# Attention of an adaLN block on one core: scores and first softmax units started inside the value projection, normalising moved to GpSimd

## What is computed

```
mod = silu(c) @ wmod                        # six vectors of 1024 for each of 4 batches
h = layernorm(x) * (1 + ca) + sa            # x is 4 x 512 x 1024
q, k, v = h @ wq, h @ wk, h @ wv            # 32 query heads, 8 key/value heads of 128
q, k = rope(q), rope(k)
scores = q k^T / sqrt(128), masked to j <= i and j > i - 256
attn = softmax(scores);  out = attn v;  x = x + ga * (out @ wo)
h = layernorm(x) * (1 + cb) + sb
x = x + gb * (top-2 of 8 experts of rank 64, summed)
```

## Time and profile before

| | |
|---|---|
| median of 3 runs | 2964.62 us (2964.49 to 2965.58) |
| the profiled execution, its time | 2969.41 us |
| its span in the trace | 2967.6 us |
| PE busy | 2693.1 us (91%) |
| DVE busy | 1775.6 us (60%) |
| ACT busy | 1367.0 us (46%) |
| POOL busy | 853.6 us (29%) |
| mean granted TensorE clock | 0.971 of full |

### The profile page before, as it was taken

How to read it: one execution, slowest core, us unless ns; L and a number is a source line. 1 busy time by engine, 2 the same in 40 slices (tenths; PEclk the granted TensorE clock), 3 DMA queues, 4 the chain that set the end, 5 groups by cost and what they waited for, 6 DMA issues and landing times.

```text
span 2967.6 us, 40770 instructions
## 1 busy us (share of the span) xinstructions
PE 2693.1 (91%) x12889; PEld 2169.2 (73%) x12889; DVE 1775.6 (60%) x4070; ACT 1367.0 (46%) x2753; POOL 853.6 (29%) x364
## 2 busy tenths in 40 slices
PE   5799999998799999998799999998799999998999
PEld 3477777776577777776577777776577777776777
DVE  3455656566755565656755555567855556567443
ACT  3244444545444444454444444454444444445331
POOL 2133333231333333331333333231333333332212
PEclk8799999999899999999899999999899999999999
DMA  7522221212222222122222221222222222214211
GB/s 281 191 72 71 68 67 64 71 64 87 98 71 71 71 68 67 64 70 85 93 71 71 71 71 64 69 65 88 90 71 71 71 71 67 67 64 171 85 65 57
DMA packets 140548, 245.31 MB, mean 83 GB/s; under 512 B 7440, under 2 KB 74320, under 8 KB 139216
## 3 DMA queue, kind: packets, MB, share of 16 engines
q1 hardware_dynamic: 133520, 219.49, 22.3%
q10 hardware_dynamic: 6976, 25.20, 2.3%
HBM read 227.86 MB, written 16.81 MB: 82 GB/s over the span
## 4 chain that ended last, share of the span: by engine, by line
PE 51%; DVE 21%; issue 15%; ACT 9%; DMA 2%; DVEq 1%; ACTq 0%; POOL 0%; SPq 0%; POOLq 0%
PE bank L451 16%; PE bank L453 15%; PE bank L452 15%; PE bank L500 3%; DVE swapped L722 3%; DVE rotated L725 3%; DVE rotated L720 3%; DVE prob L766 3%; ACT qo_hi L610 3%; ACT swapped L605 3%; DVE prob L750 2%; ACT prob L650 1%; DVE qo_lo L740 1%; DVE acc L873 1%; DVE pT_lo L761 1%
## 5 line engine op out<-in xcount | busy, mean ns | idle before, releaser
L431 POOL TENSOR_TENSOR w_o_lo<-stage,w_o_hi 128x1024 fp32r<-128x1024 f32 x128 | 323.7, 2529 | 652.8 <-ACT w_o_hi L426 652.8
L451 PE MATMUL bank<-hT_hi,w_q_hi 128*128 128x512 f32 x1024 | 404.0, 395 | 19.8 <-POOL w_q_lo L431 19.3
L452 PE MATMUL bank<-hT_lo,w_q_hi 128*128 128x512 f32 x1024 | 401.5, 392 | 0.0
L451 PE MATMUL bank<-w_o_hi,qo_hi 128*128 128x512 f32 x1024 | 401.3, 392 | 0.0
L453 PE MATMUL bank<-hT_hi,w_q_lo 128*128 128x512 f32 x1024 | 401.1, 392 | 0.0
L452 PE MATMUL bank<-w_o_lo,qo_hi 128*128 128x512 f32 x1024 | 400.2, 391 | 0.0
L453 PE MATMUL bank<-w_o_hi,qo_lo 128*128 128x512 f32 x1024 | 400.1, 391 | 0.0
L604 ACT ACTIVATE swapped<-bank 64x512 f32<-64x512 f32 x160 | 95.3, 596 | 623.4 <-DVE rotated L720 623.4
L431 POOL TENSOR_TENSOR w_q_lo<-stage,w_q_hi 128x1024 fp32r<-128x1024 f32 x128 | 312.4, 2452 | 194.2 <-ACT w_q_hi L426 194.2
L431 POOL TENSOR_TENSOR w_v_lo<-stage,w_v_hi 128x1024 fp32r<-128x1024 f32 x32 | 76.8, 2399 | 1009.1 <-ACT w_v_hi L426 1009.1
L650 ACT ACTIVATE prob<-prob,nbias 128x384 f32<-128x384 f32 (+2 forms) x512 | 273.5, 534 | 178.8 <-DVE nbias L750 175.3
(11 more groups left out here) (179 smaller groups left out, 5510.3 us busy)
## 6 DMA issues: line engine op xcount, KB each, us to landing
stage<-in_wq SPq DMA_DIRECT2D x128, 512.0 KB, 3.6
stage<-in_wo SPq DMA_DIRECT2D x128, 512.0 KB, 3.3
stage<-in_wk SPq DMA_DIRECT2D x33, 512.0 KB, 3.7
xb<-in_x ACTq DMA_DIRECT2D x32, 512.0 KB, 5.3
stage<-in_wv SPq DMA_DIRECT2D x32, 512.0 KB, 3.6
acc<-in_wmod SPq DMA_DIRECT2D x32, 512.0 KB, 5.9
...
```

Source lines behind the costliest of these rows:

```text
L431: eng.tensor_tensor(dst[1], src, dst[0].bitcast(F32), ALU.subtract).then_inc(s_split, 1)
L451: eng.matmul(o, st[0], mv_[0], start=start, stop=False)
L452: eng.matmul(o, st[0], mv_[1], start=False, stop=False)
```

## The change

Seven edits, in the loop and, for the first group, in the code ahead of it:

- `act_rope` starts its half copies when the projection is done, and no longer after L720. `dve_rope` waits for those copies before L720.
- The copy of weight chunk 9 moves on ACT from rotation 4 to the end of rotation 3, ahead of rotation 4's half copies.
- PE issues S(0) and S(1), five chunks of V, S(2), and the other three chunks.
- DVE does the masks of units 0 and 1 ahead of rotation 4, and their reciprocals and the mask of unit 2 inside it; ACT does the two Exps inside it.
- The multiplication by the reciprocal is issued on POOL (`pool_normalise`), after the ten weight chunks of the group.
- In `pe_attention` step u is now T(u), the K chunk if there is one, S(u + 3), and values.
- `K_AT` is (0, 1, 2, 3, 5, 7, 12, 13) in place of (1, 2, 3, 5, 7, 12, 13, 14).

The edits of the first group's code (the same calls with `early` off, masks ahead of the memset) are left out of the diff.

```diff
@@ -45,6 +45,8 @@
 LA = 3
 LAG = 3
 V_TURN = LA + 2
+EARLY = 2
+V_SPLIT = 5
 
 
 def key_tiles(i):
@@ -445,6 +453,8 @@
             with eng.Fori(0, GROUPS) as n:
                 for j in range(NC):
                     pool_chunk(eng, n, j)
+                for u in range(UNITS):
+                    pool_normalise(eng, n, u)
 
 
         def mm3(eng, o, st, mv_, start, stop):
@@ -511,12 +521,16 @@
                 m = mm3(eng, OBANK[i % 2][:], sl(v_, lambda v: v[:, kt, :]), sl(pT[i % 2], lambda p: p[:, b, :]), b == 0, b == len(kts) - 1)
             m.then_inc(s_pv, 1)
 
-        K_AT = (1, 2, 3, 5, 7, 12, 13, 14)
+        K_AT = (0, 1, 2, 3, 5, 7, 12, 13)
 
         def pe_attention(eng, n, next_k):
             for u in range(UNITS):
-                if u + LA < UNITS:
-                    pe_scores(eng, n, u + LA)
+                pe_turn(eng, n, u)
+                if u == 1:
+                    eng.wait_ge(s_act, 7 * n + 6)
+                    for t in range(QT):
+                        m = eng.transpose(bank[7][:, t * P:(t + 1) * P], swapped[1][:, t * P:(t + 1) * P], ident_t[:])
+                    m.then_inc(s_vt, 1)
                 if next_k and u in K_AT:
                     k = K_AT.index(u)
                     if k == 0:
@@ -524,12 +538,8 @@
                     m = mm3(eng, bank[0][:], sl(w_k, lambda t: t[:, k, :]), sl(hT, lambda t: t[:, k, :]), k == 0, k == KT - 1)
                     if k == KT - 1:
                         m.then_inc(s_proj, 1)
-                pe_turn(eng, n, u)
-                if u == 1:
-                    eng.wait_ge(s_act, 7 * n + 6)
-                    for t in range(QT):
-                        m = eng.transpose(bank[7][:, t * P:(t + 1) * P], swapped[1][:, t * P:(t + 1) * P], ident_t[:])
-                    m.then_inc(s_vt, 1)
+                if u + LA < UNITS:
+                    pe_scores(eng, n, u + LA)
                 if u % GQ == 1 and GQ < u < UNITS - GQ:
                     pe_values(eng, n, u // GQ - 1)
             for i in (QT - 2, QT - 1):
@@ -549,9 +559,14 @@
                 waits = {2 * q: (s_split, 10 * n + 4 + q) for q in range(4)} if h == 0 else {}
                 pe_project(eng, n, f"Q{h}", w_q, slice(h * HD, (h + 1) * HD), 1 - h % 2, waits)
             eng.wait_ge(s_wor, 8 * n + 1)
-            for u in range(LA):
+            for u in range(EARLY):
                 pe_scores(eng, n, u)
-            pe_project(eng, n, "V", w_v, slice(0, HD), 1, {})
+            bank_free(eng, n, "V")
+            for k in range(KT):
+                if k == V_SPLIT:
+                    pe_scores(eng, n, EARLY)
+                m = mm3(eng, bank[1][:], sl(w_v, lambda t: t[:, k, :]), sl(hT, lambda t: t[:, k, :]), k == 0, k == KT - 1)
+            m.then_inc(s_proj, 1)
 
         def pe_ln_chunk(eng, b1, k, bk, depth=2):
 
@@ -593,21 +608,33 @@
         OUT_STEP = {GQ * i + GQ + 1 + LAG: i for i in range(QT - 2)}
 
 
-        def act_rope(eng, n, r):
+        def act_rope(eng, n, r, early=True):
 
             slot = r % 2
-            eng.wait_ge(s_dve, 5 * n + r + 1)
+            eng.wait_ge(s_proj, 6 * n + 2 + r)
             if r >= 2:
                 eng.wait_ge(s_qk, 5 * n + r - 1)
             half = HD // 2
             bk = bank[0 if r % 2 == 0 else 1]
             eng.activation(swapped[slot][0:half, :], bk[half:HD, :], ACT.Copy)
             eng.activation(swapped[slot][half:HD, :], bk[0:half, :], ACT.Copy).then_inc(s_act, 1)
-            if r:
+            if 1 <= r < GQ:
                 act_chunk(eng, n, 5 + r)
+            if r == GQ and early:
+                for u in range(EARLY):
+                    act_exp(eng, n, u)
             dst = kt_[0][:] if r == 0 else qo[0][:, r - 1, :]
             eng.wait_ge(s_ra, 5 * n + r + 1)
             eng.activation(dst, rotated[slot][:], ACT.Copy).then_inc(s_rh, 1)
+            if r == GQ - 1:
+                act_chunk(eng, n, NC - 1)
+
+        def act_exp(eng, n, u):
+            w = P * len(key_tiles(u // GQ))
+            tile = prob[:, u % GQ, 0:w]
+            eng.wait_ge(s_msk, UNITS * n + u + 1)
+            eng.activation(tile, tile, ACT.Exp, bias=nbias[:, u:u + 1], scale=-1.0,
+                           accum_out=rowsum[:, u:u + 1]).then_inc(s_exp, 1)
 
         def act_project(eng, n, batch_done=None):
 
@@ -643,12 +670,8 @@
                     nk = len(key_tiles(i))
                     eng.activation(pT[i % 2][0][:, 0:nk, h * P:(h + 1) * P],
                                    bank[5 + u % 2][:, 0:nk * P].rearrange("p (b q) -> p b q", q=P), ACT.Copy).then_inc(s_pth, 1)
-                if s < UNITS:
-                    w = P * len(key_tiles(s // GQ))
-                    tile = prob[:, s % GQ, 0:w]
-                    eng.wait_ge(s_msk, UNITS * n + s + 1)
-                    eng.activation(tile, tile, ACT.Exp, bias=nbias[:, s:s + 1], scale=-1.0,
-                                   accum_out=rowsum[:, s:s + 1]).then_inc(s_exp, 1)
+                if EARLY <= s < UNITS:
+                    act_exp(eng, n, s)
                 if s in OUT_STEP:
                     act_outputs(eng, n, OUT_STEP[s])
             for i in (QT - 2, QT - 1):
@@ -713,16 +736,23 @@
 
         LN_VAR = 3 * QT + 1
 
-        def dve_rope(eng, n, r):
+        def dve_rope(eng, n, r, early=True):
             slot = r % 2
             bk = bank[0 if r % 2 == 0 else 1]
+            if r == GQ and early:
+                for u in range(EARLY):
+                    dve_mask(eng, n, u)
             eng.wait_ge(s_proj, 6 * n + 2 + r)
+            eng.wait_ge(s_act, 7 * n + r + 1)
             eng.tensor_tensor(rotated[slot][:], bk[:], cos_t[:], ALU.mult).then_inc(s_dve, 1)
-            eng.wait_ge(s_act, 7 * n + r + 1)
             eng.tensor_tensor(swapped[slot][:], swapped[slot][:], sin_t[:], ALU.mult).then_inc(s_rs, 1)
             eng.wait_ge(s_rs, 5 * n + r + 1)
             eng.wait_ge(s_dve, 5 * n + r + 1)
             eng.tensor_tensor(rotated[slot][:], rotated[slot][:], swapped[slot][:], ALU.add).then_inc(s_ra, 1)
+            if r == GQ and early:
+                for u in range(EARLY):
+                    dve_recip(eng, n, u)
+                dve_mask(eng, n, EARLY)
             eng.wait_ge(s_rh, 5 * n + r + 1)
             eng.wait_ge(s_ra, 5 * n + r + 1)
             hi, lo = (kt_[0][:], kt_[1][:]) if r == 0 else (qo[0][:, r - 1, :], qo[1][:, r - 1, :])
@@ -740,18 +770,29 @@
             eng.tensor_tensor(qo[1][:, :, i * P:(i + 1) * P], o, qo[0][:, :, i * P:(i + 1) * P].bitcast(F32),
                               ALU.subtract).then_inc(s_ol, 1)
 
+        def dve_mask(eng, n, u):
+            w = P * len(key_tiles(u // GQ))
+            eng.wait_ge(s_S, UNITS * n + u + 1)
+            if u >= GQ:
+                eng.wait_ge(s_T, UNITS * n + u - GQ + 1)
+            plain(eng.tensor_tensor_reduce(prob[:, u % GQ, 0:w], SBANK[u % 3][:, 0:w], mask_t[:, 3 * P - w:3 * P], -SCALE, FAR,
+                                     ALU.add, ALU.min, nbias[:, u:u + 1])).then_inc(s_msk, 1)
+
+        def dve_recip(eng, n, u):
+            eng.wait_ge(s_exp, UNITS * n + u + 1)
+            eng.reciprocal(rrow[:, u:u + 1], rowsum[:, u:u + 1]).then_inc(s_rl, 1)
+
+        def pool_normalise(eng, n, u):
+            eng.wait_ge(s_rl, UNITS * n + u + 1)
+            tile = prob[:, u % GQ, 0:P * len(key_tiles(u // GQ))]
+            plain(eng.tensor_scalar(tile, tile, rrow[:, u:u + 1], None, ALU.mult)).then_inc(s_nrm[u % GQ], 1)
+
         def dve_attention(eng, n):
-            for s in range(UNITS + LAG):
+            for s in range(EARLY + 1, UNITS + LAG):
                 if s < UNITS:
-                    w = P * len(key_tiles(s // GQ))
-                    eng.wait_ge(s_S, UNITS * n + s + 1)
-                    if s >= GQ:
-                        eng.wait_ge(s_T, UNITS * n + s - GQ + 1)
-                    plain(eng.tensor_tensor_reduce(prob[:, s % GQ, 0:w], SBANK[s % 3][:, 0:w], mask_t[:, 3 * P - w:3 * P], -SCALE, FAR,
-                                             ALU.add, ALU.min, nbias[:, s:s + 1])).then_inc(s_msk, 1)
-                if 1 <= s < UNITS + 1:
-                    eng.wait_ge(s_exp, UNITS * n + s)
-                    eng.reciprocal(rrow[:, s - 1:s], rowsum[:, s - 1:s]).then_inc(s_rl, 1)
+                    dve_mask(eng, n, s)
+                if s < UNITS + 1:
+                    dve_recip(eng, n, s - 1)
                 u = s - LAG
                 if 0 <= u < UNITS:
                     i, h = divmod(u, GQ)
@@ -760,10 +801,6 @@
                     hi, lo = (p[:, 0:nk, h * P:(h + 1) * P] for p in pT[i % 2])
                     eng.tensor_tensor(lo, bank[5 + u % 2][:, 0:nk * P].rearrange("p (b q) -> p b q", q=P), hi.bitcast(F32),
                                       ALU.subtract).then_inc(s_ptl, 1)
-                if 1 <= s < UNITS + 1:
-                    eng.wait_ge(s_rl, UNITS * n + s)
-                    tile = prob[:, (s - 1) % GQ, 0:P * len(key_tiles((s - 1) // GQ))]
```

(5 more changed lines are left out.)

7 lines of the change are left out of this document (5 added, 2 removed).

## The result

The changed kernel takes **3083.55 us** (median of 4 runs, 3081.37 to 3085.33) against 2964.6 before: 4.0% slower, a ratio of 1.040 with a 95% interval of 1.0382 to 1.0418. It was forecast 1.1% faster, 2931 us with a range up to 3003.

The account below looks back on a forecast made before the run. PE's gaps, 5.1 us a group, were laid to DVE held by POOL in the rotations and DVE's pace in the attention. Groups 17 us plus batch changes 17 us made 34 off: 2931 us, range 2897 to 3003.

Parts of the forecast that it names:

- the price X: POOL's time to multiply a 384-column unit by its reciprocal: 0.61 us estimated, between 0.41 and 1.02.
- The rotations: Query-head rotations: period stays, 6.1 before, 6.2 after; DVE's wait for POOL's L431 moves from L729 to L725.
- The handover: From rotations and V into attention: S(2)'s 1.55 us wait gone, T(0) waits 0.95; 0.8 us won of 2.5.
- the rival that I called dear: Multiplication on POOL at the two-tensor price, 1.02 us: 38 us slower, 3003 us; chance 0.25.
- The chain T(u) to T(u + 2): Attention: two units take 1.95 us plus POOL's multiplication, 0.7 more with a K between; 1.3 us a unit.
- The walk with it: Attention followed unit by unit: with T(0) and S(3), PE waits 4.4 to 4.7 us a group, 5.1 before.
- won: 0.6 us a group: Net gain forecast for each of the 28 groups that are alike, 17 us in all.
- What the chain is compared with: Attention: 1.3 us a unit for the new order's chain, hardly less than DVE's 1.33.
- The batch changes: At three batch changes PE's 14.5 us wait for L729 falls to about 8.5; 5.5 us won each, 17 in all.
- The first group: The first group, where loads of `wmod` set the pace: its change was put at nothing.
- POOL holds DVE in the attention: Rival: reciprocals, masks and `pT_lo` also wait for POOL, 3.8 us more a group, 3068 us; chance 0.05.
- the 0.80 us at which my gain was to vanish: POOL's multiplication time in the attention from which the forecast gain of 34 us is gone.

Follow-up runs that it names:

- e4: The change with POOL multiplying only the first 128 columns of each unit, the rest left unnormalised: 2979.33 us.
- e10: The kernel before with ACT's weight copies 7 to 9 moved to the ends of rotations 1 to 3 and 6 ahead of rotation 1: 2883.06 us.
- e3: The change with PE's old order in the attention and the old `K_AT`, multiplication still on POOL: 2934.6 us.
- e13: The change with DVE's reciprocal of unit s in step s, no longer in step s + 1 behind the next mask: 3036.47 us.
- e1: The change with the multiplication by the reciprocal back on DVE, PE's new order kept: 2983.25 us.
- e5: The change with PE's old order in the attention and the multiplication back on DVE: 2925.4 us.

## Why the prediction was wrong

The changed kernel's group takes 81.55 us where I had 77.1. Of these 4.45 us, 2.95 are the price X (from e4 to the change), and 1.5 are in e4 already, where X is near my own.

- **The rotations**: right. The hold moved from the old L729 to the old L725 (in rotation 4 to the old L722, as forecast): 2.77 us there and 0.69 at L759, a rotation 6.0 us as before. The Trainium skill's SBUF — State Buffer (Who interferes with whom) says that a DVE instruction with two inputs in SBUF contends with a GpSimd instruction that reads SBUF; the 2.77 us of L751 agree, and so do the rows of e10, where such pairs overlap by 0.08 us at most in rotations 1 to 4 and each takes 0.69 us.
- **The handover**: right. S(2) no longer waits. T(0) waits 0.79 us in the trace's measure, and 0.95 by the starts of the matmuls, the measure in which I had forecast 0.95.
- **The price X**: wrong, and the step that decided. I took 0.61 us, between bounds of 0.41 and 1.02, arguing that one tensor is read in place of two. Measured: 1.244. The upper bound, the price per column of the two-tensor form, was no bound. The slope from 256 to 384 columns is 2.5 ns a column against 2.16 for the two-tensor form. The mechanism of the rival that I called dear (0.25) is what happened, beyond its price: its 5.7 us per us of X times 0.63 gives 3.6 us a group over my forecast.
- **The chain T(u) to T(u + 2)**: the formula 1.95 + X was right (3.19 against 3.26 measured; with K 3.89 against 4.01). The walk with it wasn't: e4 at X = 0.63 takes 78.60 us a group, 1.5 above my 77.1. Counted by starts, PE's gaps make 5.9 us a group in e4, where I had 4.4 to 4.7. They stand where I had put them or one unit ahead, but are longer: 0.46 and 1.05 us at T(3) and T(5), 0.33 at T(7), then 0.90, 0.91, 0.71 and 0.61 at T(9), T(12), T(14) and T(15). Some 0.5 us can be e4's dearer narrow units (0.30 more for unit 3 and 0.16 for unit 5 than I had reckoned). The rest, about 1 us, is my walk's. So "won: 0.6 us a group" would have been wrong at my own prices too: some 0.4 lost, by that estimate; e4 itself loses 0.9 a group and is 0.4% slower than before.
- **What the chain is compared with**: I set 1.3 us a unit against DVE's 1.33 and concluded that nothing much was lost. I did not ask what the order had been good for. In the old order S(u + 3) stands behind T(u - 1), so the same 1.95 + X spans three units: 1.06 us a unit even at X = 1.24. The new order makes it span two, 1.6 a unit. The numbers fit (e3 against the change, e13); e13 shows that the reciprocal's place is part of it. That the span of units is the whole difference was argued, not isolated. At DVE's price the loop takes 1.95 + 0.41 = 2.36 us for two units, less than DVE's 1.33 a unit, and yet the new order costs 1.80 us a group there (e1 against e5). Only with K inside it (3.06 us, 1.53 a unit) would it bind, and no run took K out at that price.
- **The batch changes**: wrong in sign, 6.9 us lost where 17 were to be won (the parts, 5.2 and 0.6 us a time, make 5.8 and not 5.5, which changes little). I had five chunks of V run ahead of S(2). But V waits for its bank, which L748 of rotation 3 frees, and DVE comes to that at 820.83. PE row of the change:

```profile
821.56 0.80 PE L461 MATMUL bank<-hT_hi,w_v_hi 128*128 128x512 f32 x1 [10.19 <-DVE swapped L748]
```

  The wait was not removed but changed its name. I had forecast a wait of 8.5 us in place of 14.5; it is 10.2. With the old order the batch changes did win 8.3 us, half of the 17 (117.3, 117.0 and 116.0 in e3), so the loss comes with the attention that follows.
- **The first group**: put at nothing, it cost 5.7 us. The handover alone costs 0.7 (e5), with POOL's price 3.8 (e3), with the new order in its place 3.5 (e1). What these wait for was not taken apart.
- **POOL holds DVE in the attention**: rightly set low. Beside two multiplications on POOL that run from 1090.34 to 1092.80, a mask, a reciprocal and a `pT_lo` took 0.56, 0.16 and 0.54 us, as elsewhere.
- **The clock in the groups that are alike**: not in the prediction at all. It took 11 us of the 116 that the span lost.

The Trainium skill's GPSIMD Engine Reference had two figures for the price: one-input work at roughly line rate (Engine selection; 0.51 us by my estimate) and 1.8 cycles an element at best (Elementwise; 0.77 by estimate). The measured 1.244 us decides against the first for this form, whose second operand is a scalar for each partition read from SBUF, and lies far above the second, which the Trainium skill calls a best case. Both are too low, like my own number, but the second stood close to the 0.80 us at which my gain was to vanish.
